# Layer 0 of a four-layer network: three chunks of the shared network ahead of the packed experts and one behind, in the place of two and two

## The reference, cut to what matters

```python
def _L0_ffn_ref(hidden_states, gate_w, shared_gate_w, shared_up_w, shared_down_w,
                routed_gate_w, routed_up_w, routed_down_w):
    def _swiglu(x, gw, uw, dw):
        return jax.nn.silu(x @ gw) * (x @ uw) @ dw
    x = hidden_states.reshape(-1, h)
    shared_out = _swiglu(x, shared_gate_w, shared_up_w, shared_down_w)
    logits = x @ gate_w
    topk_ids = jnp.argmax(logits, axis=-1)
    topk_val = jnp.max(logits, axis=-1)
    scores = jax.nn.sigmoid(topk_val)[:, None]
    xs = x * scores
    ...
    order = jnp.argsort(topk_ids)
    sorted_x = xs[order]
    g = _grouped_mm(sorted_x, routed_gate_w, tokens_per_expert)
    u = _grouped_mm(sorted_x, routed_up_w, tokens_per_expert)
    d = _grouped_mm(jax.nn.silu(g) * u, routed_down_w, tokens_per_expert)
    ...
    return (shared_out + routed_out).reshape(b, s, h)
...
x = x + _L0_ffn_ref(_L0_cond_ref(x, cond_1024, L0_cond_weight), ...)
```

## Time and profile before

| | us |
|---|---|
| median of 3 runs | 1734.08 |
| lowest and highest of them | 1731.73, 1737.95 |
| the profiled execution, its own time | 1737.56 |
| its span in the trace | 1735.8 |
| layer 0's front jobs, TensorE's first up part to the experts' first transpose | 35.4 to 91.4 |
| the experts, to the end of the last down product | 91.4 to 289.7 |
| the rear jobs, to the first turn | 292.5 to 331.3 |
| the four turns, to the last copy | 331.3 to 338.7 |

### The profile page before, as it was taken

How to read it: one execution, slowest core, us unless ns; L and a number is a source line. 1 busy time by engine, 2 the same in 40 slices (tenths; PEclk the granted TensorE clock), 3 DMA queues, 4 the chain that set the end, 5 groups by cost and what they waited for, 6 DMA issues and landing times. The chain is left out here.

```text
span 1735.8 us, 25954 instructions
## 1 busy us (share of the span) xinstructions
PE 1482.4 (85%) x8354; PEld 1126.5 (65%) x8354; DVE 991.0 (57%) x1782; ACT 657.1 (38%) x977; POOL 426.1 (25%) x366
## 2 busy tenths in 40 slices
PE   8787888765989997897999999999967799749992
PEld 5632334633877786786888888887856677526661
DVE  5566675435644364645877776774645334447675
ACT  3175775212233332224655555553322233201110
POOL 1512221000434400010343343331007243023420
PEclk9899999967899999898999999999987899859996
DMA  5268972352223240230222202204022233245823
GB/s 188 87 255 314 343 251 93 120 170 98 92 92 101 80 143 28 76 152 4 95 101 87 111 28 101 98 19 146 1 97 85 91 109 130 67 163 186 269 90 112
DMA packets 82918, 211.38 MB, mean 122 GB/s; under 512 B 10785, under 2 KB 57762, under 8 KB 74594
## 3 DMA queue, kind: packets, MB, share of 16 engines
q1 hardware_dynamic: 66944, 166.40, 26.9%
q0 software_dynamic: 15840, 43.27, 7.4%
q10 hardware_dynamic: 2, 0.00, 0.0%
HBM read 165.21 MB, written 44.43 MB: 121 GB/s over the span
## 5 line engine op out<-in xcount | busy, mean ns | idle before, releaser
L630 POOL DMA_INDIRECT results<-sb_big,sb_s_out_row x63 | 132.4, 2101 | 466.4 <-ACT sb_big L861 304.5
L935 DVE TENSOR_TENSOR sb_h_split<-sb_big,sb_h_split 128x2048 fp32r<-128x2048 f32 x78 | 178.5, 2289 | 87.9 <-ACT sb_h_split L930 87.9
L930 ACT CAST sb_h_split<-sb_big 128x2048 fp32r x78 | 146.7, 1903 | 42.0 <-issue 40.5
L826 PE MATMUL ps<-sb_big,sb_e_hT 128*128 x624 | 141.0, 379 | 1.1 <-DVE sb_e_hT L979 1.1
L319 PE MATMUL ps<-sb_h_split 128*128 128x512 f32 x312 | 133.5, 428 | 9.6 <-DVE sb_h_split L954 6.9
L1068 DVE COPY sb_g_space<-sb_big 128x1024 f32 x168 | 108.4, 699 | 49.8 <-issue 22.8
L1068 ACT COPY sb_g_space<-sb_big 128x1024 f32 x120 | 118.5, 1048 | 41.6 <-DMA sb_big<-in_l_routed 21.2
L826 PEld LDWEIGHTS ps<-sb_big,sb_e_hT 128*128 128x128 f32 x624 | 118.2, 190 | 18.5 <-issue 1.3
L319 PE MATMUL ps<-sb_g_split,sb_g_ws 128*128 128x512 f32 x256 | 108.5, 424 | 23.4 <-DVE sb_g_product L498 15.7
L1458 POOL DMA_INDIRECT sorted_in<-sb_big,sb_p_slots x64 | 70.4, 1099 | 220.3 <-DVE sb_p_slots L1284 177.3
L321 PE MATMUL ps<-sb_h_split 128*128 128x512 f32 x312 | 124.1, 398 | 0.0
(11 more groups left out here) (450 smaller groups left out, 3210.2 us busy)
## 6 DMA issues: line engine op xcount, KB each, us to landing
sb_big<-in_l_routed SPq DMA_DIRECT2D x32, 1024.0 KB
sb_big<-in_l2f_routed SPq DMA_DIRECT2D x8, 3072.0 KB, 10.5
sb_e_wring<-in_l_experts SPq DMA_DIRECT2D x16, 1408.0 KB
sb_big<-in_l_routed SPq DMA_DIRECT2D x32, 512.0 KB
sb_big<-results SPq DMA_DIRECT2D x32, 512.0 KB, 7.2
sb_big<-sorted_in SPq DMA_DIRECT2D x18, 512.0 KB
by_token<-sb_big SPq DMA_DIRECT2D x12, 512.0 KB, 3.2
sorted_in<-sb_l1p_zero SPq DMA_DIRECT2D x2, 2048.0 KB, 9.6
```

The source lines that it names most:

```text
L630: pool.indirect_dma_start(out=results, out_offset=bass.IndirectOffsetOnAxis(ap=places.out_row[:, j:j + 1], axis=0), in_=self.tile(j), in_o ...
L826: last = pe.matmul(psum[:, 7, 0:D], self.hT[:, f // TPC, f % TPC * P:(f % TPC + 1) * P], self.weight(place, 2 * KD * self.F + f * D, D), s ...
L930: act.copy(self.own[part][:, 0, :], self.raw(e, part)).then_inc(self.own_high[part], 1)
L935: dve.tensor_tensor(self.own[part][:, 1, :], self.raw(e, part), self.own[part][:, 0, :], ALU.subtract).then_inc(self.own_low[part], 1)
```

## The change

`split` is 3. Chunks 0, 1 and 2 of the shared network stand ahead of the experts, chunk 3 behind. The order in which results are loaded, mixed and turned was written out as 2, 3, 0, 1; it is now worked out from `split` and is 3, 0, 1, 2. Of the `mix` calls, one is inside the rear job and three come at the end. The number of instructions of each engine's compute work stays the same.

```diff
-                jobs, split = [(0, 0), (0, 1), (0, 2), (0, 3)], 2
+                jobs, split = [(0, c) for c in range(NCH)], 3
+                chunk_order = tuple(range(split, NCH)) + tuple(range(split))
...
-                        for c in (2, 3, 0, 1):
+                        for c in chunk_order:
                             load_results(sp, [ctok], c, got[c])
...
-                        for count, c in enumerate((2, 3, 0, 1)):
+                        for count, c in enumerate(chunk_order):
                             pe.wait_ge(glu.added, 2 * NCH)
                             pe.wait_ge(mixed, count + 1)
                             glu.turn_result(pe, xtok, c, count)
...
-                        for count, c in enumerate((2, 3, 0, 1)):
+                        for count, c in enumerate(chunk_order):
                             glu.copy_result(act, fx, c, count)
...
                         glu.dve_jobs(dve, split, NCH, lambda n: mix(jobs[n][1], n - split))
-                        mix(0, 2)
-                        mix(1, 3)
+                        for c in range(split):
+                            mix(c, NCH - split + c)
```

## The result

| | kernel before | changed kernel |
|---|---|---|
| median of 20 runs each | 1734.47 us | 1728.60 us |
| lowest to highest | 1729.85 to 1740.51 | 1724.05 to 1735.00 |
| span of the profiled execution | 1735.8 | 1726.1 |
| longest wait of SyncE for L1068 | 32.4 | 43.8 |
| first transpose of the experts | 91.44 | 103.11 |

The ratio is 0.9965, 95% interval 0.9953 to 0.9977: 6.0 us less, 4.0 to 8.2.

A forecast was written before the change was run, and what follows sets the result against it. TensorE, busy 85% of the span, was taken as the bound, with weights pacing much of the experts' stage. Front +11.3, experts 0, rear -15.4 and clock +2.1 gave -2.0 us: 1732.1 us, range 1727.0 to 1738.0.

The forecast's parts named there:

- the front: Layer 0, chunk 0's down products to the experts: 24.9 us in place of 13.6, so experts begin 11.3 us later.
- Rival (b): Front: TensorE runs out of instructions during the gathers, making the sum +0.7 to +4.5 us; chance 0.17.
- The feature split of chunk 2: Front, ScalarE and VectorE at the head of chunk 1: costed at nothing; 1.2 us if its cover were gone.
- Part two: Experts' stage in layer 0: moves as a whole with its length kept, 0 us.
- -1.8 us for a first product at the high clock: Start of the experts' stage: gain of 1.8 us if its first product stays at the high clock.
- Rival (c): Experts' stage: the stream of weights takes up the later start, 11.3 us less lost, sum -13.3 us; chance 0.04.
- Part three: Rear of layer 0: one chunk, a 3.9 us stand, first transpose behind it 15.4 us earlier at the high clock.
- Part four: Rear's down products: the 3.9 us stand drops TensorE's clock, +2.1 us.
- rival (a): Rear: the clock stays up, sum -4.1 us, or -5.9 with the experts' first product also high; chance 0.25.
- The sum: Whole kernel: front, experts' stage, rear and clock together -2.0 us, giving 1732.1 us.

The follow-up runs named there:

- r3_before: The kernel before, unchanged, timed and traced again on a fourth chip beside the changed kernel: 1723.11 us.
- the trace of after: The changed kernel's profiled execution in the first comparison with the kernel before: span 1726.1 us, median of 20 runs 1728.60 us.
- r_before: The kernel before, unchanged, run once more for a second trace on a later chip: 1723.66 us, one run.
- r_after: The changed kernel, unaltered, run once more for a second trace on a later chip: 1725.81 us, one run.
- r3_after: The changed kernel, unaltered, against the kernel before on a fourth chip: 1720.44 us beside 1723.11, ratio 0.9984.
- r2_after: The changed kernel, unaltered, against the kernel before on a third chip: 1722.77 us beside 1724.10, ratio 1.0000.
- e1: The changed kernel with the addition of a chunk of results moved behind the rear's last subtraction: 1719.60 us, 0.9982 against the kernel before.
- e4: The kernel before with 80 unread matmuls ahead of chunk 1's down products, so the experts start later: 1735.60 us, 1.0065.
- e3: The kernel before with GpSimd's gathers held until VectorE's second addition of chunk 0: 1723.14 us, 0.9996.
- e2: The changed kernel with fifteen unread matmuls filling the rear's stand: 1720.64 us, 0.9995 against the kernel before.
- e7: The changed kernel with the addition moved behind the rear's last subtraction and ten unread matmuls in the stand: 1720.33 us, 0.9982 against the kernel before.
- e6: The kernel before with five additional VectorE operations ahead of the experts, for which TensorE waits: 1739.16 us, 1.0081.

## Why the prediction held, and where it missed

**What bounds it, the front.** Right to 0.1 us: 24.84 for 24.9, composed from rows of layer 2 and of the rear. Rival (b) fell: at 78.11 the up products start with no bracket while the gathers run. The Trainium skill (SBUF — State Buffer, Who interferes with whom) says that an operation of VectorE with at most one SBUF input, outside the 2-port modes, does not contend with GpSimd; r3_before agrees, with the addition on time at 78.94 beside gathers that end at 81.64. I had taken that rule to speak for a shortage of instructions, and TensorE had none. On VectorE and ScalarE, which were both late in the trace of after, no run tests it. What holds the addition for 1.3 to 2.7 us in two traces of fourteen is open. The feature split of chunk 2, which I had costed at nothing, did cost nothing: from TensorE's first up part to the end of chunk 0's down products are 42.4 to 43.1 us in the seven traces without it and 42.4 to 42.9 in the seven with it.

**What I compared with.** The prediction gave the front 13.6 us in the kernel before, from one trace. That fits the first comparison and only it: with the addition on time, its distances would give 16.7 - 4.7 - 13.9 = -1.9 us, and the 20 runs of each kernel exclude that with -4.0 to -8.2. By the table the change is worth, with a late addition, 11.3 - 4.7 - 13.9 = -7.3 us in layer 0; with one on time, 16.7 - 3.3 - 13.9 = -0.5 (r_before, r_after) or 16.7 - 5.0 - 13.0 = -1.3 (r3_before, r3_after). The timed runs gave -6.0 in the first comparison, 0.0 beside r2_after and -2.7 beside r3_after; r_before and r_after have one run each. The forecast of -2.0 is not far from the two later ones, but by luck: 5.4 us too few in front and 3.3 to 5.0 too many in the stage nearly cancel.

**Part two, the experts' stage.** This is the step that failed: the stage was put at 0. I wrote that it moves as a whole, on the grounds of SyncE's wait for L1068. That wait did grow as forecast, 43.8 for 43.7 us, and the stream begins with the experts. But it does not follow that the stage keeps its length; it became 4.7 us shorter in the first pair, 3.3 and 5.0 in the two others. Of these, 3.2, 1.7 and 4.7 lie between the first Silu and the last, where the stream ran denser for a reason that stays open, and 1.6, 1.7 and 0.3 are the clock of the last down products, which I had not looked at. The forecast's lower bound, -1.8 us for a first product at the high clock, had no part in it: that product ran at 0.50 again behind its stand of 2.95 us. I had weighed only the transfers ahead of the stage and not the pace in its middle. Without this term the change would have been slower than before on the later chips, by 2.8 to 3.7 us. Rival (c) had the right place and another mechanism: SyncE's longest wait grew by 11.4 us, so nothing of the 11.3 us was taken up by an earlier stream.

**Part three, the rear.** Stand 3.87 us for 3.9, the mix ahead of the last subtraction with no DMA to wait for, four chunks turned as before. With the drop taken apart it is -15.4, as forecast.

**Part four, the clock.** The direction was right, so rival (a) fell. The price was 1.5 us and not 2.1: of the two rows, 7.5 and 8.66 us, the one of layer 2 was matched, in all four traces of the changed kernel and in e1. The grounds were weak, though. I reasoned from the length of the stand alone, and e1 (2.79 us, dropped), e4 (2.64, dropped) and the earlier trace rows (2.64, held) show that it decides nothing between these.

**The sum.** -2.0 forecast, -6.9 read at the end of layer 0 and -6.0 measured: the miss is the 4.7 us of part two and 0.6 from part four, less 0.4 by which chunk 0 ended later. The condition that I had set for being wrong, a stage that changes by more than 2 us, was met, while the time itself stayed in the range, 1.6 us above its lower end. The range reaches down there for rival (a), which did not come true, so that was luck. Layer 1 changed by 2.7 us in the same pair, which scatter explains as well.

## What to carry to other kernels

Moving work from behind a long stage to in front of it trades one stand for another, and both were composed here from rows of the same pattern elsewhere in the trace to 0.1 us, the clock apart. A stand in one trace is not yet a property of the kernel: see whether it comes again on another chip before it is counted as a gain, since here 5.4 of 7.3 us were of that kind. And a stage that starts as a whole need not keep its length where its transfers set the pace; give it a term of its own, of both signs, and before two lengths of it are compared, take out what the clock did at its ends.

## What the runs showed of the hardware

- The same kernel took 1734.5 us in the first comparison and 1722.3 to 1724.1 us on three other occasions, each on its own chip: more than the change is worth.
- In the two traces of the first comparison a VectorE addition was held for 1.3 and 2.7 us beside GpSimd's gathers in layer 0, and another for 3.5 and 4.9 us beside its indirect DMAs in layer 2, with nothing in the trace that they wait for; ScalarE was late beside three of the four. In twelve other traces this never came, beside the same work of GpSimd in all but e3's layer 0.
- Down products behind stands of 2.64 to 3.87 us ran in 6.0 us (clock 1.00), 7.5 (0.72) or 8.67; with fifteen and with ten matmuls of 512 columns in the stand (e2, e7) the clock stayed at its upper level.
- The stream of weights ran at 353 to 381 GB/s in the same part of the work, with the same loads in the same order; a delay of 17 us by VectorE (e6) left the whole stage 0.1 us shorter and the part between its Silus 1.1 us shorter than in r3_before.
